# The second MLP with sign matrices in float32r and activations in two float32r parts

## The reference

```python
def _binarize(w):
    alpha = jax.lax.stop_gradient(jnp.mean(jnp.abs(w), axis=1, keepdims=True))
    bw = alpha * jnp.sign(w)
    return w + jax.lax.stop_gradient(bw - w)
bw1 = _binarize(w1)                                # (1024, 256)
h = jnp.einsum('bsd,hd->bsh', x, bw1) + b1
h = jax.nn.gelu(h, approximate=False)
bw2 = _binarize(w2)                                # (256, 1024)
out = jnp.einsum('bsh,dh->bsd', h, bw2) + b2
```

## Time and profile before

| | us |
|---|---|
| median of three runs | 4287.51 |
| span of the profiled execution | 4290.7 |
| PE busy | 3633.3 (85%) |
| PE weight loads | 2042.8 (48%) |
| DVE busy | 2510.6 (59%) |
| ACT busy | 1932.9 (45%) |
| POOL busy | 1495.8 (35%) |

### The profile page before, as it was taken

How to read it: one execution, slowest core, us unless ns; L and a number is a source line. 1 busy time by engine, 2 the same in 40 slices (tenths; PEclk the granted TensorE clock), 3 DMA queues, 4 the chain that set the end, 5 groups by cost and what they waited for, 6 DMA issues and landing times. The chain is left out here.

```text
span 4290.7 us, 59366 instructions
## 1 busy us (share of the span) xinstructions
PE 3633.3 (85%) x19241; PEld 2042.8 (48%) x19241; DVE 2510.6 (59%) x6732; ACT 1932.9 (45%) x4521; POOL 1495.8 (35%) x1807
## 2 busy tenths in 40 slices
PE   7378779987899879998799978998899988998787
PEld 2245444554446534465445544465444644455433
DVE  6754757366663667446573666536674575736652
ACT  5123435545254444554355542544445543545433
POOL 4133441254323451234422543234512444235311
PEclk8589899999899989997999988999899988999888
DMA  6210230002300231002300023002310023001120
GB/s 233 70 33 13 58 104 14 13 27 56 92 16 22 53 81 42 14 12 60 102 14 24 21 55 87 15 22 53 88 34 15 12 60 102 14 24 30 46 65 6
DMA packets 230687, 203.85 MB, mean 48 GB/s; under 512 B 11457, under 2 KB 212417, under 8 KB 230346
## 3 DMA queue, kind: packets, MB, share of 16 engines
q1 hardware_dynamic: 226338, 190.51, 15.9%
q0 software_dynamic: 3328, 8.39, 0.7%
q10 hardware_dynamic: 720, 1.15, 0.1%
HBM read 121.73 MB, written 77.69 MB: 46 GB/s over the span
## 5 line engine op out<-in xcount | busy, mean ns | idle before, releaser
L2330 ACT ACTIVATE arena<-pb 128x512 f32<-128x512 f32 (+3 forms) x1536 | 671.5, 491 | 342.6 <-PE pb L1565 337.5
L2410 POOL TENSOR_TENSOR arena<-arena,small 128x512 f32<-128x512 f32 x256 | 288.0, 1127 | 463.4 <-DVE small L1740 462.0
L2159 ACT ACTIVATE arena<-arena,small 128x256 f32<-128x256 f32 x512 | 256.0, 500 | 394.9 <-DVE small L1723 388.3
L2574 POOL TENSOR_SCALAR_AFFINE_SELECT arena<-arena 128x256 f32<-128x256 f32 x512 | 220.5, 433 | 544.7 <-ACT arena L2330 542.6
L1582 PE MATMUL pb<-arena,v 128*17 128x512 f32 (+3 forms) x3072 | 365.7, 506 | 32.9 <-POOL arena L2574 24.1
L2014 DVE TENSOR_REDUCE arena<-pb 128x1 f32<-128x512 f32 x512 | 329.8, 682 | 90.6 <-PE pb L1540 89.7
L1565 PE MATMUL pb<-arena 98*128 98x512 bf16 (+3 forms) x1152 | 355.3, 343 | 9.4 <-ACT arena L2330 5.7
L1723 DVE CUSTOM_DVE_ANT_0 arena<-pb,wmask 128x256 f32<-128x256 f32 x512 | 195.8, 419 | 218.5 <-PE pb L1282 218.3
L1282 PE MATMUL pb<-arena 128*128 128x256 f32 x1024 | 283.0, 401 | 5.4 <-issue 4.0
L1259 PE MATMUL pb<-hTf,wqkv 128*128 128x512 f32 (+1 forms) x640 | 245.8, 536 | 22.6 <-DVE hTf L1692 10.8
L1660 PE MATMUL pb<-xh,w1T 128*128 128x512 f32 x512 | 251.8, 640 | 9.7 <-DVE xh L1880 8.6
(11 more groups left out here) (354 smaller groups left out, 7588.8 us busy)
## 6 DMA issues: line engine op xcount, KB each, us to landing
arena<-split_q SPq DMA_DIRECT2D x64, 384.0 KB, 4.3
arena<-split_k SPq DMA_DIRECT2D x24, 768.0 KB, 7.1
split_q<-arena SPq DMA_DIRECT2D x64, 192.0 KB, 2.3
split_q<-arena SPq DMA_DIRECT2D x96, 128.0 KB, 2.0
split_k<-arena SPq DMA_DIRECT2D x64, 192.0 KB, 2.4
split_k<-arena SPq DMA_DIRECT2D x96, 128.0 KB, 2.1
arena<-split_k SPq DMA_DIRECT2D x24, 384.0 KB, 5.7
xn<-h_d SPq DMA_DIRECT2D x8, 1024.0 KB
```

What stands on the lines that cost most here:

```text
L2159: ins = s.activation(pm[n % 3][:, j], sm[n % 2][:, j], ACT.Exp, bias=nmx[:, 2 * sl + j:2 * sl + j + 1], scale=-1.0, accum_out=sml[:, 2 * s ...
L2330: s.activation(pp[pn % 4][:, h % 2, 0:w_], bank[n % 3][:, 0:w_], ACT.Exp).then_inc(a_exp1, 1)
L2410: g.tensor_tensor(pm[n % 3], pm[n % 3], rcl[:, 2 * sl:2 * sl + 2].unsqueeze(2).broadcast_to([P, 2, 2 * P]), ALU.mult).then_inc(p_norm0, 1)
L2574: g.affine_select(out=p2, in_=p2, pattern=[[0, 2], [1, P]], compare_op=ALU.is_ge, fill=0.0, base=0, channel_multiplier=-1).then_inc(p_tri, 1)
```

## The change

- The weights are sign matrices in float32r (`w1T`, `w2T` turned from the bf16 signs directly). The row factors alpha go elsewhere: that of w1 into the scale of the GELU instruction, that of w2 into the gate row (`gate_rows`, two more DVE operations at the end of the pick part, alpha sent through DRAM).
- bias times gate is made once for all batches in the same place and loaded by DMA (`load_last_gate`); POOL's multiplication in `add_bias` is gone.
- Activations are split: `xr` (hi part and lo part of the normalised half) and `gr` (hi and lo of one eighth of the hidden width, two buffers). The hi part is a copy to float32r, the lo part the difference.
- The first product is 4 matmuls of 128x512 per m, into banks (6, 7) for c=0 and into bank 7 alone for c=1. GELU writes `gf[m % 2]`.
- The second product is done per eighth m of the hidden width, 8 matmuls of 128x256, two steps after first product m; it accumulates over all m in two banks. Steps 18 to 21 hold the gated additions, steps 22 and 23 nothing.
- For c=0 the lo part of `gr` is made on POOL, for c=1 on DVE; the hi part on DVE for both.
- A gate in `schedule()` is added; the list `ORDER` of steps comes out as before.

```diff
-        MLP1_BANKS = {0: (6, 7), 1: (7, 5, 6)}
+        MLP1_BANKS, MLP1_OUT = {0: (6, 7), 1: (7, 5)}, {0: (0, 1), 1: (5, 6)}
+        FIRST_BANKS = {0: (6, 7), 1: (7,)}
...  PE
-                    for m in range(FT):
-                        bk = banks[m % len(banks)]
+                    def first(m):
+                        bk = FIRST_BANKS[c][m % len(FIRST_BANKS[c])]
                         for w in left[bk]:
                             t.wait_ge(*w)
-                        for k in range(KD):
-                            mm = t.matmul(bank[bk], w1T[:, k, m * P:(m + 1) * P], hT2[:, k], start=k == 0, stop=k == KD - 1)
+                        for part in range(2):
+                            for k in range(KD):
...
+                                mm = t.matmul(bank[bk], w1T[:, k, m * P:(m + 1) * P], xr[:, part, k], start=part + k == 0, stop=part + k == 2)
                         mm.then_inc(t_w1, 1)
                         left[bk] = [(a_g, FT * H + m + 1)]
...
+                    def second(m):
...
+                        t.wait_ge(v_ghi, FT * H + m + 1)
+                        if c:
+                            t.wait_ge(v_glo, FT * b + m + 1)
+                        else:
+                            t.wait_ge(p_glo, FT * b + m + 1)
+                        for i in range(TH):
+                            ob = bank[MLP1_OUT[c][i // 2]][:, (i % 2) * D:(i % 2 + 1) * D]
+                            for part in range(2):
+                                mm = t.matmul(ob, gr[:, m % 2, part, i * P:(i + 1) * P], w2T[:, m], start=m + part + i % 2 == 0,
+                                              stop=m == FT - 1 and part == 1, skip_group_check=True)
...
+                    for m in range(FT + 2):
+                        if m < FT:
+                            first(m)
+                        if m >= 2:
+                            second(m - 2)
+                        yield
...  DVE, norm_half
+                    v.wait_ge(v_n2, 4 * H + 1)
+                    v.tensor_copy(xr[:, 0, 1], hT2[:, 1]).then_inc(v_n2, 1)
+                    yield
+                    v.wait_ge(a_n2, 2 * H + 2)
+                    v.tensor_tensor(xr[:, 1, 0], hT2[:, 0], xr[:, 0, 0], ALU.subtract).then_inc(v_n2, 1)
+                    v.wait_ge(v_n2, 4 * H + 2)
+                    v.tensor_tensor(xr[:, 1, 1], hT2[:, 1], xr[:, 0, 1], ALU.subtract).then_inc(v_n2, 1)
...  DVE, mlp1
+                    def split(m):
+                        v.wait_ge(a_g, FT * H + m + 1)
+                        if m >= 2:
+                            v.wait_ge(t_wg, (FT - 1) * H + m - 1)
+                        v.tensor_copy(gr[:, m % 2, 0], gf[m % 2]).then_inc(v_ghi, 1)
+                        if c:
+                            v.wait_ge(v_ghi, FT * H + m + 1)
+                            v.tensor_tensor(gr[:, m % 2, 1], gf[m % 2], gr[:, m % 2, 0], ALU.subtract).then_inc(v_glo, 1)
...  ACT
-                    if c == 0:
-                        s.wait_ge(split_out[1][0], 16 * SPLIT_DMAS * (b + 1))
                     for m in range(FT):
                         s.wait_ge(t_w1, FT * H + m + 1)
+                        if m >= 2:
+                            if c:
+                                s.wait_ge(v_glo, FT * b + m - 1)
+                            else:
+                                s.wait_ge(p_glo, FT * b + m - 1)
                         gelu_tables[0] = True
-                        s.activation(g1[:, m], bank[banks[m % len(banks)]], ACT.Gelu,
+                        s.activation(gf[m % 2], bank[FIRST_BANKS[c][m % len(FIRST_BANKS[c])]], ACT.Gelu, scale=cols[:, C_AL + m:C_AL + m + 1],
                                      bias=cols[:, C_FB1 + m:C_FB1 + m + 1]).then_inc(a_g, 1)
...  POOL
-                    add_bias(b, c, rows[:, R_B2:R_B2 + D], gates[:, 3])
-                    for _ in range(FT):
+                    add_bias(b, c)
+                    for m in range(FT + 2):
+                        if c == 0 and 1 <= m <= FT:
+                            g.wait_ge(v_ghi, FT * H + m)
+                            g.tensor_tensor(gr[:, (m - 1) % 2, 1], gf[(m - 1) % 2], gr[:, (m - 1) % 2, 0], ALU.subtract).then_inc(p_glo, 1)
                         yield
...  pick part: DVE and POOL
-                        v.scalar_tensor_tensor(out=wtmp[m % 2][:, 0:width], in0=sgn[:, c0:c0 + width], scalar=ac, in1=w, op0=ALU.mult,
-                                               op1=ALU.subtract).then_inc(b_sign, 1)
...
-                for m, (w, width, _) in enumerate(BINARY):
-                    g.wait_ge(b_sign, m + 1)
-                    g.tensor_tensor(w, w, wtmp[m % 2][:, 0:width], ALU.add).then_inc(b_add, 1)
```

More of the change, by code:

```diff
@@ L10 @@
 BF16 = mybir.dt.bfloat16
+F32R = mybir.dt.float32r
 I32 = mybir.dt.int32
@@ L148, in turn @@
         if key[0] == "mlp1" and key[2] == 0 and n == 1 and not reached([(("att", key[1], 0), steps_of(("att", key[1], 0)))]):
+            return
+        if key[0] == "att" and key[2] == 1 and n == len(first_fills(1)) + 1 and not reached([(("mlp1", key[1], 0), 24)]):
             return
@@ L1045, in _ @@
                             s.wait_ge(b_turn, n + 1)
-                            s.activation(dst, bank[6 + n % 2][:, 0:nn * P].rearrange("p (c q) -> p c q", q=P), ACT.Copy).then_inc(b_take, 1)
+                            s.activation(dst, bank[6 + n % 2].bitcast(BF16)[:, 0:nn * P].rearrange("p (c q) -> p c q", q=P), ACT.Copy).then_inc(b_take, 1)
                 s.wait_ge(c_to_act, NITER)
@@ L1184, in adaln_kernel @@
         lane = [Lane(j) for j in range(2)]
-        g1, xn2m = at(arena, ZONE_B, [FT, NH]), at(arena, ZONE_B + FT * NH, [TH, D])
+        xn2m = at(arena, ZONE_B + FT * NH, [TH, D])
         hT2 = xh[:, :].rearrange("p (k n) -> p k n", k=KD)
+        gf = [hT2[:, i] for i in range(2)]
         xadd2 = [at(arena, HB + 2832 + i * D, [D]) for i in range(2)]
@@ L1430, in norm_half @@
                         mm.then_inc(t_n2, 1)
[L1431 removed]
+                        left[bk] = [(v_n2, 4 * H + 1) if k else (a_n2, 2 * H + 2)]
                         yield
@@ L1661, in mlp1 @@
                         mm.then_inc(t_w1, 1)
                         left[bk] = [(a_g, FT * H + m + 1)]
[L1663 to L1678 removed]
+                    def second(m):
+                        if m == 0:
+                            for bk in MLP1_OUT[c]:
+                                for w in left[bk]:
+                                    t.wait_ge(*w)
+                        t.wait_ge(v_ghi, FT * H + m + 1)
[8 more added lines that the diff above has]
+                                              stop=m == FT - 1 and part == 1, skip_group_check=True)
+                            if m == FT - 1:
+                                mm.then_inc(t_w2, 1)
+                            elif i == TH - 1:
+                                mm.then_inc(t_wg, 1)
+                        if m == FT - 1:
+                            for i, bk in enumerate(MLP1_OUT[c]):
+                                left[bk] = [(v_w2, TH * H + 2 * i + 2)]
@@ L1679, in mlp1 @@
+                    for m in range(FT + 2):
[3 more added lines that the diff above has]
+                            second(m - 2)
+                        yield
+                    for _ in range(6):
                         yield
@@ L2251, in norm_half @@
                     s.wait_ge(t_n2, 2 * H + 1)
-                    s.activation(hT2[:, 0], bank[banks[0]], ACT.Identity, scale=modc[:, 5 * KD, b:b + 1], bias=modc[:, 4 * KD, b:b + 1]).then_inc(a_n2, 1)
+                    for dst in (xr[:, 0, 0], hT2[:, 0]):
+                        s.activation(dst, bank[banks[0]], ACT.Identity, scale=modc[:, 5 * KD, b:b + 1], bias=modc[:, 4 * KD, b:b + 1]).then_inc(a_n2, 1)
                     yield
```

119 lines of the change are left out of this document (58 added, 61 removed).

## The result

The changed kernel takes 4315.66 us (median of 4 runs, 4310.84 to 4319.32), the kernel before beside it 4289.57: a ratio of 1.0055, 95% interval 1.0041 to 1.0068. It is slower by 0.55%, where a gain of 0.2% was the likeliest case. The time lies within the stated range (4215 to 4345), but above case (A)'s own (4255 to 4300).

The account below looks back on a forecast made before the run. PE was taken to bound the products before, the chain through ACT, DVE and POOL after. 4290.7 - 29.4 - 9.9 + 42 - 8 - 3.5 = 4281.9 us profiled, less 3.2 gives 4279; range 4215 to 4345.

Parts of the forecast that it names:

- case (A): The prediction's own case, all terms as worked out: 4279 us, own range 4255 to 4300, chance 0.40.
- the queue on DVE behind the last second product of c=0: In mlp1(b, 0), gated products and fills' reductions left on DVE before the row of five reductions: 6.2 us.
- the path of c=1 at full clock: In mlp1(b, 1), longer rounds against second products no longer behind the scores, lost cover included: -0.1 us a stage.
- Pick part: POOL's additions go, two DVE operations fall from 1.90 to 0.28 us; with the sign operations -3.5 us.
- c=0, batches 0 to 6: mlp1(b, 0): POOL's subtractions and gathers bound, DVE's five reductions begin earlier; 4.2 us a stage, -29.4 for seven.
- c=0, batch 7: mlp1(7, 0): no gathers between, PE and handovers set the pace, 23.9 us instead of 33.8: -9.9.
- c=1: mlp1(b, 1), batches 0 to 6: -0.1 us at full clock and 6.1 for half clock, +6.0 a stage, +42 for seven.
- Tail: mlp1(7, 1), alone at the end: 18.7 us instead of 26.6, so -8.
- (B): Rival: the clock holds in c=1, which gives -1 instead of +42 us: 4236, chance 0.17.
- (C): Rival: exposed float32r weight loads or dearer passes, 1.5 to 1.7 us a product, not 0.85: 4343; 0.22 with half-clock case.
- (E): Rival: DVE and POOL exclude each other, c=0's period grows about 0.5 us, +25 for seven stages: 4304, chance 0.16.
- (D): Rival: PE bounds the stages after all and the 240 us come, less the fills' share: some 4100, chance 0.05.

Follow-up runs that it names:

- e4: The changed kernel with twenty more 128x256 matmuls before each c=1 first product that waits for a group's first GELU, batches 0 to 6; 4286.07 us.
- e3: The changed kernel with the low parts of c=0 made by DVE instead of POOL, which keeps only the gathers; 4285.76 us.
- e7: The changed kernel with sign matrices and both parts of the activations in bfloat16 instead of float32r; 4296.26 us.
- e6: The kernel before, all in float32, with the first product of c=1 going into bank 7 only; 4407.83 us.
- e1: The changed kernel with the second product of eighth m-2 ahead of the first product of eighth m in c=1; 4276.54 us.

## Why the prediction was wrong

Its mechanisms were the right ones and the sum of their sizes was off by 34.6 us of span (4281.9 against 4316.5), every large term to the same side. Two steps failed above all: the queue on DVE behind the last second product of c=0 (6.2 us taken, 7.6 measured, and half clock behind it), and the path of c=1 at full clock (-0.1 us a stage taken, about +2.2 by e4). Of the cases named, the one with the clock at half nearly all through (4302) comes nearest to 4315.66, but the clock was far from half all through.

- **Pick part**: -3.5 forecast, -3.3 from its begin to its end (the 0.7 before it is setup). Right; the operation of 1.90 us is back at 0.28 (`138.10 0.28 DVE L913`).
- **c=0, batches 0 to 6**: -29.4 forecast, -14.8 measured: 14.6 us of the miss. The POOL part held: low part at +3.9 as forecast, the last second product's end forecast at +23.6, measured 1123.97 + 1.03 - 1101.27 = +23.7. The term that was mis-sized is what is queued behind it on DVE: 6.2 us taken, 7.6 measured in this stage (1125.00 to 1132.62). I had taken the busy time of DVE from a window; but reductions and PE's fills wait for each other in turn there, and two of the operations between them lasted 0.70 and 0.77 us beside a POOL addition, before 0.32 and 0.35. That is 1.4 us a stage. Another 0.8 a stage was lost behind the row's begin, at half clock (the windows above), where the prediction had the stage "DVE's, as before" and no part for the clock. POOL as the bound was forecast rightly; e3 shows that this choice of engine alone held back 23 us.
- **c=0, batch 7**: -9.9 against -6.9. Ten steps of 1.7 us were 1.88, 1.8 of the 3.0 us: the price of float32r was put at the rows' 0.85 us a product. The rest is not traced.
- **c=1**: +42.0 against +53.1, 11.1 us. In `mlp1(1, 1)` the rounds up to the fourth unit came out about as worked: 25.5 us at full clock, 26.1 in e4, and 31.6 with the clock's part, measured 1351.96 - 1321.33 = 30.6. The step that failed is the end: 10.9 us for the next four units, 12.2 in e4 at full clock, 14.5 measured. The last second product waited 1.79 us (2.01 in e4) for its low part, which DVE makes behind the unit's softmax and beside a POOL operation, and in the changed kernel it ran at half clock again with the scores behind it; the prediction had no clock's part there. Over all stages the full-clock path was underrated by about 2.3 us a stage and the clock's share, 6.1, lay above the 5.4 that e4 leaves: two errors of opposite sign, so the 42 is nearer to 53.1 than its terms earned.
- **Tail**: -8 against -6.0 at PE's last instruction and about -4 in all. That it is so near is luck. The stage before was read too short: 26.6 us from the chain of the earlier trace rows, which counts 48 of the 64 records of the second product, where PE's timeline has 16.26 + 13.98, about 30.1 us to the last matmul's end. And the stage now was forecast at 18.7 us and took 4303.44 + 1.03 - 4280.95 = 23.5. Its first products ran at half clock, with a wait of 0.87 us at each GELU behind the norm's wait of 5 us, and the full clock came only after second products stood between; and four gated additions stand behind the end, before one.

The second product of the tail before, the tail's products after (PE's timeline), and a window after:

```profile
4266.84 13.98 PE L1673 MATMUL pb<-w2T,arena 128*128 128x256 f32 x64
```
```profile
4284.40 2.08 PE L1674 MATMUL pb<-xr,w1T 128*128 128x512 f32 x4 [0.87 <-ACT xh L2423]
4289.22 1.91 PE L1691 MATMUL pb<-w2T,gr 128*128 128x256 f32 x8
```
```profile
4284.00:4293.00 9.00, 7.73 (x22) 6.04 (x23) 3.36 (x6) 2.04 (x4) 0.00 (x0) 0.50 0.00 0
```

- **GELU**: 0.78 us for 0.69, on each round and the tail. This was to be had beforehand. The changed GELU takes a scale from a column, and ACT's rows of the norm, with scale and bias from columns, already had 0.78 before (L2252 at 4248.97). The Trainium skill, "ScalarE: Activation LUTs", What ACT_TABLE_LOAD costs, gives 93 ns for each such operand; the trace agrees (781 - 686 = 95 ns).

Of the rivals, (B) is refuted: the clock did fall in c=1. (C), dearer passes or exposed loads, was a small truth, 8 to 12% of a product and not a factor of two. (E) was right on the mechanism and wrong on the price: copies last 1.30 us beside a POOL subtraction, but are over (1109.18) before the gather behind that subtraction is (1110.02), and cost the period nothing. The Trainium skill, "SBUF — State Buffer", SBUF: two separate sides, also says that fast DVE copies keep GpSimd from writing descriptors. In e3 most gathers kept 0.94 us and their pitch of 1.25 beside such copies. One took 1.16, but so did one of the kernel before (1.15), which has no such copies in this stage; so no lock of a copy's length shows in the gathers' issue. (D) failed as argued.

The common error is how the open costs were set: handovers, a dearer type, a queue at the end can only add to a chain of waits, and I had set all but the clock's share at their lower end.

## What to carry to other kernels

When PE is made cheaper in a stage where another engine is as full as PE (ACT here, 17.41 of 18.60 us), much of the saved time turns into waits, and most waits of 3 us cost a second time by the clock. Decide first where the cheaper work will stand: inside the other engine's busy phase, not between its phases. And when banks are taken for accumulation, count which first products now wait for their reader before pricing the matmuls.

## What the runs showed of the hardware

- float32r on 128x128 stationary tiles: 0.93 us for four matmuls of 512 columns and 0.95 for eight of 256 (e3), bfloat16 0.87 for eight of 256 (e7), float32 3.51 for eight of 256. Weight loads of the second product take 210 ns on the mean with float32r (half clock included), 190 with float32 (before) and 106 with bfloat16.
- PE waits of 3.0 to 3.6 us in the c=1 stages were followed by half clock, for some 3 to 8 us, in 18 of 21 cases in the changed kernel and 16 of 21 in e6. Waits of 0.92 to 1.11 us behind twenty matmuls (e4) never were. Of e1's fourteen waits of 1.38 us, four fell at half clock. In the tail the granted clock stayed at 0.50 from 4284 to 4293 us while first products with waits of 0.87 us between them ran.
- A GpSimd subtraction of 128x512 took 1.29 us with float32r output and 1.16 with bfloat16, and lengthened a DVE copy beside it from 0.43 to 1.30 us.
